# A graph layer's message kernel: the weighting of the gates moved from VectorE to POOL, and four gate components added by one VectorE operation

## The reference

```python
s1 = concat([xs[:, :8], xd[:, :8]]); v1 = concat([xs[:, 8:], xd[:, 8:]])      # 16 scalars, 16 vectors
vdot1 = einsum('euk,ek->eu', v1, sh1) / sqrt(3)
s_t = a1 * (s1 . Wss + vdot1 . Wvv);  v_t = a1 * ((s1 . Wsv) sh1 + v1 . Wvs)   # W = MLP(emb), per edge
vdot2 = einsum('euk,ek->eu', v_t, sh1) / sqrt(3)
scal, gates = a2 * (s_t . Ass + vdot2 . Avv), a2 * (s_t . Bss + vdot2 . Bvv)
vecs = a2 * ((s_t . Csv) sh1 + v_t . Cvs)
edge_out = concat([tanh(scal), vecs * tanh(gates)]) * norm                     # norm: the edge's weight
x = layernorm(x + segment_sum(edge_out, dst))
```

## Time and profile before

| | |
|---|---|
| median of three runs | 785.0 us |
| the profiled execution | 785.59 us, span 783.4 us |
| PE busy | 672.7 us (86%) |
| DVE busy | 728.3 us (93%) |
| ACT busy | 552.9 us (71%) |
| POOL busy | 536.4 us (68%) |
| longest group | L335 POOL gathers x416, 405.4 us |
| largest on DVE | L728 and L690, 238.2 and 238.1 us, x104 each |
| chain that ended last | PE 60%, DVE 29%, issue 7% |

### The profile page before, as it was taken

How to read it: one execution, slowest core, us unless ns; L and a number is a source line. 1 busy time by engine, 2 the same in 40 slices (tenths; PEclk the granted TensorE clock), 3 DMA queues, 4 the chain that set the end, 5 groups by cost and what they waited for, 6 DMA issues and landing times.

```text
span 783.4 us, 20601 instructions
## 1 busy us (share of the span) xinstructions
PE 672.7 (86%) x6667; PEld 306.0 (39%) x6770; DVE 728.3 (93%) x1321; ACT 552.9 (71%) x1279; POOL 536.4 (68%) x655
## 2 busy tenths in 40 slices
PE   0788889999998999899998999899999998999874
PEld 0533434443444444343444434344444434443323
DVE  8389999999999999999999999999999999999964
ACT  2267777777777777877787777777777777777731
POOL 8577877688767877687768776887688767876100
PEclk9699999999999999999999999999999999999998
DMA  3321111111111111111112111111111111111000
GB/s 103 92 61 21 45 28 38 24 43 27 39 28 44 28 25 37 44 28 28 40 24 44 26 39 24 47 28 39 21 45 28 34 28 37 27 25 24 11 1 22
DMA packets 36099, 27.34 MB, mean 35 GB/s; under 512 B 14326, under 2 KB 34448, under 8 KB 35994
## 3 DMA queue, kind: packets, MB, share of 16 engines
q1 hardware_dynamic: 21646, 18.15, 8.1%
q0 software_dynamic: 13312, 6.84, 5.9%
q10 hardware_dynamic: 1036, 1.02, 0.4%
HBM read 21.77 MB, written 4.20 MB: 33 GB/s over the span
## 4 chain that ended last, share of the span: by engine, by line
PE 60%; DVE 29%; issue 7%; DMA 1%; ACT 1%; POOL 0%; DVEq 0%; SPq 0%; POOLq 0%
DVE z_s L728 13%; PE ps L957 12%; PE ps L894 10%; PE ps L878 8%; DVE p_s L690 7%; PE ps L937 6%; PE ps L866 4%; PE ps L912 4%; PE ps L858 3%; PE ps L885 3%; PE ps L950 2%; PE ps L925 2%; PE ps L944 2%; PE ps L968 1%; DMA x_dram<-eo_all 1%
## 5 line engine op out<-in xcount | busy, mean ns | idle before, releaser
L335 POOL DMA_INDIRECT xs<-in_xp,src_i x416 | 405.4, 974 | 111.7 <-issue 105.5
L728 DVE TENSOR_TENSOR z_s<-ps,h 128x2048 f32<-128x2048 f32 x104 | 238.2, 2290 | 10.5 <-PE ps L912 1.2
L690 DVE TENSOR_TENSOR p_s<-ps,h 128x2048 f32<-128x2048 f32 x104 | 238.1, 2289 | 5.9 <-PE ps L957 5.9
L483 ACT CAST v_s<-ps 128x512 bf16<-128x512 f32 x312 | 181.4, 581 | 48.6 <-PE ps L878 45.3
L957 PE MATMUL ps<-f,w_f 32*128 32x512 f32 x832 | 120.5, 645 | 50.3 <-DVE z_s L728 32.0
L878 PE MATMUL ps<-p_s,sum_m 128*32 128x512 f32 x832 | 110.8, 601 | 15.3 <-DVE m L744 8.4
L894 PE MATMUL ps<-z_s,w_z 128*32 128x512 f32 x832 | 110.8, 605 | 3.8 <-DVE z_s L728 2.5
L446 ACT COPY oht<-ps 42x512 bf16<-42x512 bf16 x104 | 60.3, 580 | 68.6 <-PE ps L858 68.6
L377 POOL TENSOR_TENSOR along<-fe,r 128x192 f32<-128x192 f32 x104 | 58.6, 564 | 56.7 <-ACT fe L464 50.7
L452 ACT COPY f<-ps 128x512 f32<-128x512 f32 x104 | 61.0, 586 | 41.1 <-PE ps L866 41.1
L937 PEld LDWEIGHTS ps<-ident,u 128*128 128x128 f32 x416 | 43.6, 140 | 86.4 <-issue 86.4
(11 more groups left out here) (115 smaller groups left out, 890.8 us busy)
## 6 DMA issues: line engine op xcount, KB each, us to landing
emb<-e_dram SPq DMA_DIRECT2D x309, 30.0 KB
xs<-in_xp,src_i POOLq DMA_INDIRECT x416
e_dram<-e_part SPq DMA_DIRECT2D x7, 360.0 KB, 3.2
e_in<-in_emb SPq DMA_DIRECT2D x8, 240.0 KB
window<-x_dram SPq DMA_DIRECT2D x104, 7.9 KB
x_dram<-eo_all SPq DMA_DIRECT2D x1, 585.9 KB
eo_all<-in_vec_t SPq DMA_DIRECT2D x1, 528.0 KB, 3.6
xt_n<-in_xt SPq DMA_DIRECT2D x1, 400.0 KB, 3.7
```

Of the source, the lines that this page charges most:

```text
L335: nc.gpsimd.indirect_dma_start(xs_r[n][:, t, :], None, xp, bass.IndirectOffsetOnAxis(src_i[:, m * T + t:m * T + t + 1], axis=0)).then_inc( ...
L483: nc.scalar.copy(v_s[:], v_ps).then_inc(v_step, 1)
L690: nc.vector.tensor_tensor(p_s[:], ps[:, 0:4, :], h1_r[m % 2][:].unsqueeze(1).to_broadcast([128, 4, BE]), ALU.mult).then_inc(p_done, 1)
L728: nc.vector.tensor_tensor(z_s[:], ps[:, 0:4, :], h2_r[k % 3][:].unsqueeze(1).to_broadcast([128, 4, BE]), ALU.mult).then_inc(z_done, 1)
```

## The change

`gated` goes from VectorE's list to POOL's; VectorE's `outputs(k)` waits for its semaphore `weighed` as before. `gate_sums` is one reduction over the four components. In `gates` the 96-wide product comes first. `hidden_2` stands at the start of the step it belongs to, on PE behind `repeat`, on ACT first of all. The loop ends at step NB, and the last blocks are written out by hand, with fewer warming matmuls. The copy of x in DRAM, which the windows are loaded from, is laid out part by part and stored in three DMAs. A few gathers and one early copy (`misfits`) change places in the start. In the diff the pieces stand in this order: the loop's range, SP, POOL, ACT, VectorE (gates, sums, the loop, the last blocks), PE.

```diff
-        STEPS = range(-5, NB + 6)
+        STEPS = range(-5, NB + 1)
...
             sp.wait_ge(zeroed, 1)
-            sp.dma_start(x_dram[N:N + WIN, :], no_rows[:]).then_inc(x_stored, 16)
-            sp.wait_ge(x_part_ready, PARTS)
-            sp.dma_start(x_dram[0:N, :].rearrange("(p m) c -> p m c", p=P), x_part.rearrange("p m n c -> p m (n c)")
-                         ).then_inc(x_stored, 16)
+            sp.dma_start(x_dram[:, N:N + WIN, :].rearrange("n m c -> m n c"), no_rows[:]).then_inc(x_stored, 16)
+            for n in range(PARTS):
+                sp.wait_ge(x_part_ready, n + 1)
+                sp.dma_start(x_dram[n, 0:N, :].rearrange("(p m) c -> p m c", p=P), x_part[:, n, :, :]).then_inc(x_stored, 16)
...
+            def gated(k):
+                gates = eo_all[:, k, :, 0:16]
+                pool.wait_ge(tanh_done, k + 1)
+                if k == 0:
+                    pool.wait_ge(wgt_loaded, 16)
+                nc.gpsimd.tensor_tensor(gates, gates, wgt_s[:, T * k:T * k + T].unsqueeze(2).to_broadcast([128, T, 16]),
+                                        ALU.mult).then_inc(weighed, 1)
...
                         if real(i + 3):
                             directions(i + 3)
+                        if real(i - 4):
+                            gated(i - 4)
                         later_emb(i)
                         if real(i + 5):
                             gather(i + 5, 3, T)
+
+            for k in range(NB - 3, NB):
+                gated(k)
...
             for i in STEPS:
+                if real(i):
+                    hidden_2(i)
                 if real(i):
                     part_of_v(i, 0)
...
-                if real(i + 1):
-                    hidden_2(i + 1)
                 later_emb(i)
...
-                r = r4[:, T * k:T * k + T, :].unsqueeze(3).to_broadcast([128, T, 4, 16])
-                nc.vector.tensor_tensor(m1[:], e_ps[:, :, :, 0:16], r, ALU.mult).then_inc(fin_step, 1)
                 r = r4[:, T * k:T * k + T, 1:4].unsqueeze(3).to_broadcast([128, T, 3, 8])
...
                 nc.vector.tensor_tensor(m4[:], e_ps[:, :, 0:1, 16:24].to_broadcast([128, T, 3, 8]), r,
                                         ALU.mult).then_inc(vec_step, 1)
+                r = r4[:, T * k:T * k + T, :].unsqueeze(3).to_broadcast([128, T, 4, 16])
...
+                nc.vector.tensor_tensor(m1[:], e_ps[:, :, :, 0:16], r, ALU.mult).then_inc(fin_step, 1)
                 dve.wait_ge(vec_step, k + 1)
...
             def gate_sums(k):
-                dve.wait_ge(fin_step, 2 * k + 1)
-                nc.vector.tensor_tensor(m2[:], m1[:, :, 0:2, :], m1[:, :, 2:4, :], ALU.add).then_inc(fin_step, 1)
-                dve.wait_ge(fin_step, 2 * k + 2)
-
-                nc.vector.tensor_tensor(gsc[:], m2[:, :, 0, :], m2[:, :, 1, :], ALU.add).then_inc(gsc_done, 1)
+                dve.wait_ge(fin_step, k + 1)
+                if k >= 1:
+                    dve.wait_ge(tanh_done, k)
+                nc.vector.tensor_reduce(gsc[:], m1[:].rearrange("p t g u -> p t u g"), AX.X, ALU.add).then_inc(gsc_done, 1)
...
-                if real(i - 4):
-                    gated(i - 4)
...
+            a, b, c, d = range(NB - 4, NB)
+            gates(c)
+            gate_sums(c)
+            outputs(b)
+            gates(d)
+            base = base_of(a)
+            gate_sums(d)
+            outputs(c)
+            accumulate(a, base)
...
                 if real(i - 1):
                     repeat(i - 1)
+                if real(i):
+                    hidden_2(i)
                 if real(i):
                     sum_1(i)
...
-                if real(i + 1):
-                    hidden_2(i + 1)
...
+            keep_warm(2)
+            over_nodes(NB - 4)
+            turn(NB - 1)
...
+            over_nodes(NB - 3)
+            nodes_themselves()
+            over_nodes(NB - 2)
+            keep_warm(4)
+            over_nodes(NB - 1)
+            keep_warm(4)
```

More of the change, by code:

```diff
@@ L73, in program @@
         w_z = sb("w_z", [128, 2, D])
-        no_rows = sb("no_rows", [WIN, PARTS * D], BF16)
+        no_rows = sb("no_rows", [WIN, PARTS, D], BF16)
         src_i = sb("src_i", [128, TILES], I32)
@@ L87, in program @@
         e_dram = nc.dram_tensor("e_dram", (PARTS, NB * HID, BE), BF16, kind="Internal").ap()
-        x_dram = nc.dram_tensor("x_dram", (N + WIN, PARTS * D), BF16, kind="Internal").ap()
+        x_dram = nc.dram_tensor("x_dram", (PARTS, N + WIN, D), BF16, kind="Internal").ap()
         xs_r = [sb(f"xs{n}", [128, T, D]) for n in range(4)]
@@ L108, in program @@
         m1 = sb("m1", [128, T, 4, 16])
-        m2 = sb("m2", [128, T, 2, 16])
         gsc = sb("gsc", [128, T, 16])
@@ L128, in program @@
         x_rest = early(P, NT * D).rearrange("p (m c) -> p m c", m=NT)
-        x_part = early(P, PARTS * NT * D // 2).bitcast(BF16).rearrange("p (m n c) -> p m n c", n=PARTS, m=NT)
+        x_part = early(P, PARTS * NT * D // 2).bitcast(BF16).rearrange("p (n m c) -> p n m c", n=PARTS, m=NT)
         vt = early(128, 3 * TILES).rearrange("p (e k) -> p e k", k=3)
@@ L396, in _ @@
             gather(0, 3, T)
-            gather(1, 0, T)
-            gather(2, 0, 1)
+            gather(1, 0, 3)
             pool.wait_ge(r4_ready, 1)
@@ L403, in _ @@
                 for i in STEPS:
+                    if i == -4:
+                        gather(1, 3, T)
                     if real(i + 3):
@@ L406, in _ @@
                         directions(i + 3)
+                    if real(i - 4):
+                        gated(i - 4)
                     if i == -3:
-                        gather(2, 1, T)
+                        gather(2, 0, T)
                     if real(i + 4) and i + 4 >= 3:
@@ L525, in _ @@
                     act.wait_ge(x_rest_ready, n)
-                nc.scalar.copy(x_part[:, :, n, :], xt_s if n == 0 else x_rest).then_inc(x_part_ready, 1)
+                nc.scalar.copy(x_part[:, n, :, :], xt_s if n == 0 else x_rest).then_inc(x_part_ready, 1)
                 if n < 2:
@@ L566, in _ @@
                     nc.scalar.activation(nrm_t[:, TA:TILES], n2_t[:, TA:TILES], ACT.Sqrt).then_inc(norm_ready, 1)
+            copy_one_hot(NB - 3)
+            tanhs(NB - 2)
+            copy_one_hot(NB - 2)
+            tanhs(NB - 1)
+            copy_one_hot(NB - 1)
             nc.scalar.activation(warmed[:], warm[:], ACT.Sqrt)
@@ L653, in _ @@
             link(nc.vector.tensor_copy(w_first[:], w1_s))
+            dve.wait_ge(misfit_sum, 1)
+            nc.vector.tensor_copy(misfits[:], ps[0:1, 7, 0:1]).then_inc(misfits_ready, 1)
             link(nc.vector.tensor_tensor(w1_s, w1_s, w_first[:], ALU.subtract))
@@ L703, in accumulate @@
                 nc.vector.tensor_tensor(nodes, nodes, node_ps, ALU.add).then_inc(acc_done, 1)
-            def gated(k):
-                gates = eo_all[:, k, :, 0:16]
-                dve.wait_ge(tanh_done, k + 1)
-                if k == 0:
-                    dve.wait_ge(wgt_loaded, 16)
-                nc.vector.tensor_tensor(gates, gates, wgt_s[:, T * k:T * k + T].unsqueeze(2).to_broadcast([128, T, 16]),
-                                        ALU.mult).then_inc(weighed, 1)
             def outputs(k):
@@ L789, in _ @@
                             ins.then_inc(r4_step, 1)
+            a, b, c, d = range(NB - 4, NB)
[7 more added lines that the diff above has]
+            accumulate(a, base)
+            base = base_of(b)
+            accumulate(b, base)
+            flag = dve.value_load(misfits[0:1, 0:1], min_val=0, max_val=EP)
+            outputs(d)
+            for k in (c, d):
+                base = base_of(k)
+                accumulate(k, base)
             with dve.If(flag):
@@ L901, in over_nodes @@
                     pe.wait_ge(ohs_ready, k + 1)
+                    pe.wait_ge(acc_done, k)
                 pe.wait_ge(h2_ready, min(k + 6, NB))
@@ L977, in _ @@
             for i in STEPS:
+                if i == -4:
+                    turn_one_hot(0)
                 if real(i - 1):
                     repeat(i - 1)
+                if real(i):
+                    hidden_2(i)
                 if real(i):
@@ L999, in _ @@
                     first_layer(i + 1)
-                if real(i + 4):
+                if real(i + 4) and i + 4 >= 1:
                     turn_one_hot(i + 4)
```

25 lines of the change are left out of this document (8 added, 17 removed).

## The result

The changed kernel takes 1000.3 us (median, 996.6 to 1004.9) where the kernel before, on the same chip, takes 784.75: 1.275 times as long, 95% interval 1.270 to 1.281. A repeat gave 1003.6 against 785.8, ratio 1.279 (1.274 to 1.283). The forecast was 982 with a range of 946 to 1030. The profiled execution took 999.8 us, its span 997.9, with a mean granted clock of 0.899.

A forecast was written before the change was run, and what follows sets the result against it. A loop of waits through ACT and POOL was to set the step, 8.56 us instead of VectorE's 6.85: 785.6 - 667.9 + 830.3 + 25.9 + 3 - 5.5 - 2 + 13 = 982.4 us, range 946 to 1030.

The forecast's parts named there:

- the loop and its embedding steps: Waits from p_s through ACT, POOL and outputs to next p_s: 97 x 8.56 = 830.3 us, plus 25.9 for embedding.
- TensorE's clock: PE's idle gaps lower its clock: 0.6 us for each of 16 long gaps and a few others, 13 us.
- the start: Storing x in three parts, with smaller window-load pieces behind, takes 2 us off (5 off to 3 on).
- the end: Last block's sum to last accumulate, 12.4 us before, some 6.5 without PE's other work: 5.5 off (0 to 7).
- What bounds, and that POOL's turn decides: Outputs would wait for POOL some 100 times, 1.5 us or so each; L377's start against outputs' turn decides.
- The six steps of the loop: Gate products 2.99, L878 3.13, ACT's copies 6.48, POOL's directions then weighting 7.50 to 7.75, outputs 7.83, p_s 8.56 us.
- The embedding steps: POOL's embedding rests wait for ACT, making 16 steps late by 1.62 us each: 25.9 us.
- Nothing for VectorE's removed work: VectorE's saved 0.1 to 0.3 us a step falls before a wait: booked nothing; without cover up to 29 us.
- hidden_2 behind the repeat: On PE, moving it costs nothing; its gain, z_s 0.20 us earlier, lies beside the loop.
- The rival with a fall in half of the steps: Half-size variant of the rival that the clock falls in most steps: 1018 us; that rival's chance 0.15.
- the 1066: Rival that TensorE's clock falls in most steps, 1.0 us in 97 steps: 1066 us; chance 0.15.
- The rival that POOL is in time: POOL's weighting ready before outputs wants it, PE's loop bounds at 6.56 us a step: 750 us; chance 0.06.

The follow-up runs named there:

- filled kernel: Changed kernel plus seven idle 128x128 identity products a step on PE behind the turn of the features, steps 4 to 101: 962.1 us, ratio 1.226.
- the move alone: Kernel before with only the weighting moved to POOL, behind directions: 1023.1 us, ratio 1.303; in the first group of runs 1.023.
- best version: Changed kernel with the weighting first in POOL's step, the rests of the embedding later and the two additions back: 761.0 us, ratio 0.970.
- the rest of the change: Changed kernel with the weighting put back on VectorE, all other parts kept: 761.3 us, ratio 0.971.
- the weighting first: Changed kernel with POOL's weighting moved ahead of the gathers and directions in its step: 766.2 us, ratio 0.975.

## Why the forecast was right, and where its terms were off

Measured against the sum, all from profiled executions: forecast 982.4; the loop and its embedding steps with 3 us of set-up, 859.2 forecast and 849.3 in the filled kernel, -9.9; TensorE's clock, 13 booked and 887.3 - 849.3 = 38.0 found, +25.0; the start, 2 booked and 3.9 found (p_s of step 4 at 62.29), -1.9; the end, 5.5 booked and 1.1 found (48.3 us behind the p_s of step 101, 49.4 before), +4.4; what lies around the span, -0.3. That makes 999.7 of 999.8. The 9.9 us too much in the loop hid part of the 25.0 too little in the clock; that the two stood against each other is luck. With the loop alone right it would have been 972, 27 us short in place of 17.

- *What bounds, and that POOL's turn decides.* Right. Outputs waits for POOL 97 times, as foretold, though for 2.6 us on average and 2.02 in the undisturbed step, not 1.5: the prediction's own times (sums through before 6, outputs at 7.83) leave over 1.8. L377's start behind outputs' turn in the earlier trace rows was the right row: the move alone gives 1.303, and the same product put first in POOL's order gives 0.975.
- *The six steps of the loop.* From p_s at 497.44: L909 3.08 (3.13), L481's end 6.42 (6.48), POOL 6.50 (6.56), weighting 7.44 (7.50), outputs 7.76 (7.83), p_s 8.46 (8.56). 0.05 us less up to the sum, and 0.03 less from outputs on. POOL's 128x64 product takes 0.29 us; the slope through the earlier trace rows had given 0.25, and the estimate by the Trainium skill's factor of two ("GPSIMD Engine Reference", section "4.1 Engine selection") 0.44. The trace decides against the factor for this size: VectorE needs 0.22 for the same product, 0.29 is 1.3 times that.
- *The embedding steps.* Predicted 10.2, measured 10.1 and 10.02. L522 starts 9.85 us after the p_s of the step before (497.44 to 507.29), as worked out, and POOL's rest at 10.55.
- *Nothing for VectorE's removed work.* Right in the kernel as it is, as outputs waits after the sums are through; wrong in its aside, that without this cover it would be worth up to 29 us. The reduction takes 0.58 us, not at most 0.48, and saves nothing against two additions; the weighting holds VectorE for 0.14; and PE's first_layer is late next: p_s comes 3.63 us after z_s, and it was 3.64 in before. The prediction's own way over PE (2.44 + 1.14 + 0.08 = 3.66) is no shorter than that, so its rows already spoke against the 29: in the earlier trace rows first_layer ends at 459.44, 0.06 ahead of p_s, as in the best version, and VectorE did not set the step alone. The best version tried shows 0 instead of 29.
- *hidden_2 behind the repeat.* "What it would give lies beside the loop" held; with the loop gone it is worth 0.22 us a step, the larger part of what the rest of the change gains (15.3 us in the 77 ordinary steps, of 25.0 between the profiled executions).
- *The clock.* The mechanism was right, the term was mis-sized: 13 us booked, 38.0 found. I booked losses for the 16 embedding gaps and few others; it is the other way round. The embedding steps lose nothing, since POOL covers a slow sum, and 37 of 77 ordinary steps lose about 1 us each: 686.0 - 651.0 = 35.0 us in these steps, and 3.2 more in steps 6 to 9. The gap was forecast well, 1.9 against 1.70 measured; what failed was the belief that an ordinary gap would seldom do what a long one does. The earlier trace rows had shown one fall, and I took it for the mark of long gaps. The rival with a fall in half of the steps had 1018, at 1.0 us each in 49 steps. What it named against itself, that a fall makes PE later and so closes the gap before the next one, is in the rows: 24 of the 25 gaps of 0.93 to 1.55 us stand behind a step whose sum was slow, and none of the 25 was followed by a slow one. The Trainium skill ("TensorE: Matmul & The Clock Gate", section "HAM oscillation — how this bites in real kernels") describes a kernel in which each of its waits, of some 3 to 5 us, put the clock down again. The gaps here are shorter, so that the 1066 that the prediction took from the page does not follow from it. By the trace the sign holds, and not every gap costs: 37 of the 52 gaps of 1.66 to 1.79 us were followed by the lower clock.
- *The end.* Over-booked: from the last block's sum L925 to the last accumulate 10.2 us are left of 12.4, not some 7, and ahead of and behind this stretch the end is 0.6 us longer each. PE's timeline of the end, and VectorE's last accumulate:

```profile
974.62 1.06 PE L925 MATMUL ps<-z_s,w_z 128*32 128x512 f32 x8 [2.37 <-DVE z_s L742]
...
979.75 0.28 PE L936 MATMUL ps<-ohs,eo_all 128*32 128x42 f32 x8 [2.21 <-DVE acc L725]
979.97 2.87 PE L1006 MATMUL ps<-xt_n,centre 32*32 32x400 f32 x16
...
983.07 1.33 PE L1000 MATMUL ps<-ident 128*128 128x128 f32 x8
```

```profile
984.78 0.20 DVE L725 TENSOR_TENSOR acc<-acc,ps 128x42 f32 x1 [1.28 <-PE ps L936]
```

The nodes' own product (2.87 us) and the warming ones (1.33) still lie between the last blocks in PE's order (in before there were 24 warming products among them, not 20). And a new wait came in: PE's `over_nodes` of block 101 stands idle for 2.21 us until VectorE has accumulated block 100, which VectorE's new list puts behind the gates of the last block. The prediction had counted PE's other work alone.
- *The rival that POOL is in time* did not happen, but its kernel exists: the weighting first. Its 750 us is 766 measured: 6.63 a step where 6.56 was worked out (7 us; from p_s to z_s it is 2.99, not 2.90), the waits at the embedding steps (16 steps, 116.8 us in place of 16 x 6.63 = 106.1), and 3 us less gained at the end; against that, the 3 us of set-up were not found and the start gained 2 more.

## What to carry to other kernels

Before an operation goes to an engine with room, find out when that engine reaches its turn, not how busy it is: the price is the latest input of whatever stands ahead of it in the queue, and who waits behind the result. Here POOL had a quarter of its time in the loop free (in before it was busy for 443 of the 600 us from 100 to 700) and the moved operation 0.29 us of work; its place in the order was worth 237 us. And ask what is late next on the engine that is relieved: a matmul that ended 0.03 us after VectorE's tail made the relief worth nothing.

## What the runs showed of the hardware, unexpected

- The reduction of 256 to 64 elements with strided reads takes 0.58 us on VectorE, the one of 192 to 64 takes 0.36: two additions over the same data (0.28 and 0.22) are not slower.
- Gaps of 1.6 to 1.8 us in PE's work were followed by a lower clock in 37 of 52 ordinary steps (34 of 55 in the repeat), gaps of 0.9 to 1.6 us in none of 25 (22), and with 1.73 us of products that nobody reads in the gap in none of 77: 38 us of 1000 won by work that computes nothing.
- The same program, the kernel before, took 785, 1010 and 1051 us in different groups of runs; in the groups with 1010 and 1051 results of PE were taken up late. The record gives the same chip number, 13, for the group with 1051 and for a later one with 785.8, so it is not the chip alone. Ratios moved as well: the move alone 1.023 there and 1.303 here. The cause stays open.
